# Placing the first instruction of the attention and convolution loops at slot 0 of a fetch line, on every engine

## The reference

```
x = x + attention(gn(x))     # 8x8 windows, 4 heads of 32, keys from the 12x12 around each window,
                             # relative position terms, mask that keeps every second row and column
x = x + conv3x3(gn(x)) + bias   # 128 -> 128 channels, over tiles that aren't all (nearly) zero

qkv = einsum('bchw,oc->bohw', x, W_qkv)
attn = softmax(q k^T + rel_pos_emb(q) + FIXED_MASK)
out = einsum('bchw,oc->bohw', attn v, W_out)
```

## Time and profile before

| | us |
|---|---|
| median of three runs | 3842.27 |
| the profiled execution | 3843.86 |
| its span, first to last instruction | 3842.0 |
| PE busy | 3535.2 |
| DVE busy | 3338.5 |
| ACT busy | 2977.3 |
| POOL busy | 2575.5 |

### The profile page before, as it was taken

The page is one execution under the profiler, slowest core; times in us unless marked ns, Lnnn a source line. Parts: engine busy times, 40 slices in busy tenths (PEclk is TensorE's granted clock), DMA queues, the critical chain, the costliest instruction groups (busy, mean ns, idle before and its releaser), DMA issues. The chain is left out here.

```text
span 3842.0 us, 136271 instructions
## 1 busy us (share of the span) xinstructions
PE 3535.2 (92%) x51718; PEld 2514.5 (65%) x51718; DVE 3338.5 (87%) x5626; ACT 2977.3 (77%) x5320; POOL 2575.5 (67%) x3344
## 2 busy tenths in 40 slices
PE   0799999999999999999999999999949999999999
PEld 0577777777877777777777777778724444444444
DVE  9699999999988888888888888889879888888887
ACT  0788888888988888887888888789657777777774
POOL 1677777777767777776777777677646666666664
PEclk9999999999999999999999999999979999999999
DMA  8344444443333333333333333333234333343332
GB/s 360 82 127 153 138 139 153 128 149 101 96 91 84 94 94 84 99 93 86 85 94 98 83 96 93 85 85 98 75 123 161 147 153 153 147 152 153 151 151 87
DMA packets 492422, 463.06 MB, mean 121 GB/s; under 512 B 9664, under 2 KB 469312, under 8 KB 469440
## 3 DMA queue, kind: packets, MB, share of 16 engines
q1 hardware_dynamic: 491968, 455.92, 36.9%
HBM read 321.40 MB, written 134.48 MB: 119 GB/s over the span
## 5 line engine op out<-in xcount | busy, mean ns | idle before, releaser
L1003 POOL TENSOR_TENSOR sb_tf<-sb_cf 128x1024 f32<-128x1024 f32 x256 | 609.4, 2382 | 393.2 <-DVE sb_tl L985 371.0
L482 PEld LDWEIGHTS ps_s<-sb_kf,sb_qb 128*64 128x64 f32 x16384 | 534.4, 141 | 262.2 <-issue 247.2
L482 PE MATMUL ps_s<-sb_kf,sb_qb 128*64 128x54 f32 x16384 | 601.6, 228 | 91.3 <-issue 88.9
L462 PE MATMUL ps_t<-sb_ident,sb_d 128*108 128x128 f32 x4096 | 671.7, 287 | 8.7 <-ACT sb_pt L650 4.4
L612 DVE TENSOR_TENSOR sb_qb<-ps_q,sb_own_head 128x1024 f32<-128x1024 f32 x512 | 620.6, 1212 | 14.4 <-PE ps_q L444 14.4
L911 PE MATMUL ps_c<-sb_th,sb_wc_h 128*128 128x512 f16 x1536 | 584.7, 381 | 40.3 <-DVE sb_tl L985 40.3
L731 POOL TENSOR_TENSOR sb_erel<-sb_brel 128x288 f32<-128x288 f32 x512 | 351.7, 687 | 375.1 <-DVE sb_brel L559 374.3
L911 PE MATMUL ps_c<-sb_th,sb_wc_l 128*128 128x512 f16 x1536 | 583.8, 380 | 0.0
L911 PE MATMUL ps_c<-sb_tl,sb_wc_h 128*128 128x512 f16 x1536 | 583.7, 380 | 0.0
L738 POOL TENSOR_TENSOR sb_d<-sb_scores,sb_srcp 128x288 f32<-128x288 f32 x512 | 342.8, 670 | 318.3 <-PE ps_t L462 159.3
L761 POOL TENSOR_TENSOR sb_zl<-sb_zf,sb_zh 128x396 f16<-128x396 f32 x512 | 481.2, 940 | 83.7 <-ACT sb_zh L714 82.3
(11 more groups left out here) (117 smaller groups left out, 8258.4 us busy)
## 6 DMA issues: line engine op xcount, KB each, us to landing
sb_xb<-rows SPq DMA_DIRECT2D x128, 780.0 KB, 6.1
sb_xc<-x SPq DMA_DIRECT2D x64, 1280.0 KB, 5.4
sb_x<-rows SPq DMA_DIRECT2D x128, 512.0 KB, 4.0
x<-sb_x SPq DMA_DIRECT2D x128, 512.0 KB, 3.2
out<-sb_oc SPq DMA_DIRECT2D x64, 1024.0 KB, 3.9
sb_abuf<-rows SPq DMA_DIRECT2D x16, 2048.0 KB, 12.4
sb_st<-rows SPq DMA_DIRECT2D x32, 1024.0 KB, 8.6
sb_raw<-wconv SPq DMA_DIRECT2D x1, 576.0 KB, 4.1
```

What stands on the lines that cost most here:

```text
L462: last = pe.transpose(ps_t[0:KV, wj * 128:(wj + 1) * 128], d[:, at:at + KV], ident[:])
L482: last = pe.matmul(s_at, qb[:, qc:qc + QB], kf[:, kc:kc + KR], start=True, stop=True)
L1003: pool.tensor_tensor(tf[:, k * TF:(k + 1) * TF], view(cf, 0, 128, c0 + ra * W, [[2 * W, PAIRROWS], [1, W]]), view(cf, 0, 128, c0 + rb * W, ...
```

## The change

Both helpers pass one more argument to their loops. [...] No other instruction is added, removed or reordered. The untouched lines below it move by one or two in the file.

```diff
-                    with eng.bass.Fori(0, turns, engines=[eng.engine], hint_back_edge=True) as i:
+                    with eng.bass.Fori(0, turns, engines=[eng.engine], hint_back_edge=True,
+                                      head_slot={eng.engine: 0}) as i:
...
-                with eng.bass.Fori(0, CTURNS, engines=[eng.engine], hint_back_edge=True) as i:
+                with eng.bass.Fori(0, CTURNS, engines=[eng.engine], hint_back_edge=True,
+                                      head_slot={eng.engine: 0}) as i:
```

## The result

The changed kernel took 3731.6 us (median of 4 runs, 3729.6 to 3732.0) against 3842.2 us (4 runs, 3834.6 to 3848.4): ratio 0.9712, 95% interval 0.9694 to 0.9730. The forecast was 3720, its range 3706 to 3752. The profiled execution's span is 3729.5 us, 112.5 less than before, where the prediction had 122.5.

The account below looks back on a forecast made before the run. TensorE was taken as the bound, broken by its second-loop branch. Terms -128.3 (second loop), -4 (first loop), +8.8 (exits), +1 (entries) sum to -122.5: 3843.86 to 3721.4, less 1.6 for the profiled run: 3720 us, range 3706 to 3752.

Parts of the forecast that it names:

- What bounded the kernel: Second attention loop: TensorE sets the pace, broken only by 19 pauses at its closing branch, 87.6 us.
- the full value: Second loop, PE: all 320 groups run clean, 1544.5 us instead of 1672.8, so -128.3 us; bounds -60 and -128.3.
- The mechanism: PE's closing branch: the hinted fetch needs line time before it; slot 230 gives about 5.8 us, some 2.5 us sufficed.
- First loop, PE: First attention loop: 8.2 us of pauses before ps_o go, half counted because VectorE is as full: -4 us.
- Leaving the loops: Behind each loop's last branch PE pauses about 5.3 us; net +8.8 us over both exits, bounds +2 and +13.
- Entering: Loop entries: jumping over up to 255 empty slots once per loop and engine, +1 us in all.
- A: Line behind the head comes late, PE still pauses 1.2 us a turn: 3743 to 3781 us, middle 3755, chance 0.12.
- B: Whole kernel: nothing happens, 3842 us, chance 0.04.
- C: Both attention loops: the head's slot decides, not the branch's, so slot 0 stalls both: 3897 us, chance 0.04.
- D: First loop gives all its 8.2 us and the exits' 8.8 us hide: 3707 us, chance 0.06.

Follow-up runs that it names:

- PE alone: Changed kernel with heads at slot 0 on TensorE only, the other four engines as before the change: 3726.9 us, ratio 0.9683.
- slot 4: Changed kernel with TensorE's head at slot 30 in both attention loops, so both closing branches stand 4 instructions into their line: 3882.1 us, ratio 1.0085.
- no hint: Changed kernel without the back-edge hint on TensorE's two attention loops, heads still at slot 0: 3876.8 us.
- all but PE: Changed kernel with heads at slot 0 on every engine except TensorE: 3850.0 us, ratio 1.0002.
- slots 40, 60, 100: Three runs: changed kernel with TensorE's second-loop head at slot 40, 60 or 100: 3851.3, 3853.6 and 3807.6 us.
- the load first: Changed kernel with SyncE issuing the sb_st load ahead of the sb_xb load: 3701.5 us, ratio 0.9626; with slot 0 on TensorE only, 3698.7 us.
- second loop only: Changed kernel without head_slot on the first attention loop; the second and the convolution keep it: 3732.5 us, ratio 0.9698.
- before with the load first: Kernel before the change with only the sb_st load issued ahead of the sb_xb load: 3832.0 us, ratio 0.9960.
- PE's second loop only with the load first: Changed kernel with only TensorE's second-loop head at slot 0 and the sb_st load issued ahead of sb_xb: 3716.4 us, ratio 0.9660.

## Why the prediction was right, and the term that failed

**What bounded the kernel: right.** In the second loop PE was the bound and its branch the only break. Removing the 19 pauses gave 128.1 us, where the sum had 128.3 (1672.8 less 1544.5). 87.6 us of it are the pauses, and 40.7 follow them: the 32 passes behind a pause took 1.96 us instead of 1.14 and the first group 6.99 instead of 4.83, and the windows view has the granted clock at 0.50 from 1061.3 to 1064.7 us. The assumption behind the full value, that neither VectorE nor ScalarE would take over, held: no wait of PE for another engine from 991 to 2536 us.

**The mechanism: right, its reading of time too simple.** PE alone carries it; slot 4 brings it into the first loop; no hint brings it into both. The head's packet starts 4.8 us ahead of the branch at slot 230 and 2.5 us behind it at slot 4, and a late branch ends some 2.5 us after that start, the time that the prediction had read from one exit. That the hint gets the head fetched ahead is shown by the pair with the branch at slot 230: 4.81 us ahead of it with the hint, 2.42 us behind it without. A taken branch took 4.93 and 6.04 us without the hint, 5.0 us with the hint and 4 to 34 instructions into its line, and 0.45 and 0.36 us with 96 and 230. But the prediction's wording that 230 instructions give "5.8 us against some 2.5 us" suggested a price that falls evenly from slot 0 on. It stays at 5.0 us up to 34 instructions.

**The step that failed: "First loop, PE ... I count half: -4".** It measured +5.9, 9.9 of the 10 us by which the sum missed. The 8.2 us of ps_o pauses went, and gave nothing: with PE alone at slot 0 the loop took 659.7 us against 659.3. I had argued from the busy shares that VectorE was as full as PE, and split the difference. The waits would have told it: VectorE itself lay idle 24.3 us for `sb_st` in that loop, and with its busy time that is all but 5.5 us of the loop. Held by VectorE and its transfer, this loop gave nothing for a shorter PE. With the load moved, the same slot gave 14 to 24 us. So the gain was there and hidden behind the transfer.

**The +6 itself** stays open. In the rows it is VectorE's wait for `sb_st`, 30.6 us instead of 24.3. With the other engines' heads at slot 0 (changed kernel, all but PE, slots 40, 60, 100) the first loop took 665.2, 668.1, 658.9, 662.2 and 661.3 us, and 659.3, 659.7 and 661.0 where they were not. The means, 663.1 and 660.0, are no further apart than single executions scatter. One candidate is SyncE, which issues `sb_st`: at the loop's entry its first hint starts at 232.9 us instead of 229.2. It does not explain the 6 us by itself. In the runs with slots 40, 60 and 100 that hint starts at 232.9 to 233.5 too, and the waits for `sb_st` are 24.2, 27.6 and 26.7 us. In medians the other engines' slots cost 2.8 us with the load first (3701.5 against 3698.7).

**Leaving the loops: right in kind, sizes exchanged.** Forecast was a pause of 5.3 us at each exit; measured 4.96 and 3.30. The first exit was to count +1.5 of it, but the written-out units took 5.3 us more, PE's own 2.8 us of longer pause among them; with PE alone at slot 0 they took 3.9 more. VectorE did not hide it. Behind the second loop it was +3.8 instead of +7.3. There the fetch of the next line started 2.54 us after the last branch, and 3.78 behind the first loop; the prediction had taken 4.0 for both, from the first loop's exit. The clock was granted at 0.50 behind either (902 to 908 and 2540.2 to 2543.5 us). Both with the entries: +9.5 against 9.8, so that the exits and entries came out right in sum by luck.

**Entering: +1 forecast, +0.4 measured ahead of the first loop,** but not for every slot. No run shows the empty slots of the prediction's +1; what the runs show is the jump, one branch more per padded loop. It has a price of its own: 0.31 us from about slot 164 or 194, 0.6 to 2.8 us from about slot 122 (the first loop's entry, nine runs), 5.14 and 6.18 us from about slot 30. That the changed kernel's second jump stands at slot 164 is luck; the bounds of the prediction, three pauses of 5, had room for it.

**The rivals.** A, a late line behind the head, did not come: ps_s starts 77.24 us apart over the back edge. Its margin was wider than the half microsecond of the prediction, since in the second loop the line behind the head is fetched 2.1 to 3.7 us after the branch (median 2.5), which makes it usable after some 5.0 us and not 6.6. (The prediction puts A's middle at 3755; the middle of 3743 and 3781 is 3762. And 128.3 us over 19 pauses are 6.75, not 6.6. Neither moves the forecast.) B fell with the result. C, the head's slot decides, fell with slots 30 to 100: the price goes away as the branch moves deeper into its line, and slot 0, which C would have made the worst head, is the best. Head and closing branch move together in these runs; the jumps into the second loop, 0.31 and 6.18 us to the same slot 0, separate the two, though for a jump without hint. D needed the first loop's 8.2 us.

## What to carry to other kernels

Where a loop body is fetched anew in every turn (here 12 or 13 packets a turn), count the instructions from the start of the fetch line to its closing branch on the engine that sets the pace; up to 34 the branch hint bought nothing here, at 74 a third of the branch's time, at 96 two thirds to nearly all. The head's slot is then the cheapest thing to move (here on PE alone; the other engines' heads gained nothing and cost 2.8 us). Look at the slot of the jump into the loop as well, which moves with every head ahead of it (here from slot 30 to 164, and from 6.18 to 0.31 us). A gain in one loop says nothing of the next: before giving a pause's removal a value, look in that loop's waits for who is last, transfers included. After such a change read the loops again; here a load issued ahead of another was worth twice as much as it had been before.

## What the runs showed of the hardware

- PE's taken branch with hint, by instructions between its line's start and the branch: 4, 14 and 34 took 5.0 us (medians 5.04, 4.97, 5.05), 74 took 3.33, 96 took 0.45 in the first loop before, 230 took 0.36. Without hint it was 4.93 in the second loop and 6.04 in the first. At 96 it varied most between runs, with medians of 0.45, 0.63, 0.99, 1.39 and 1.61 us (before, second loop only, all but PE, before with the load first, PE's second loop only with the load first). In the last two the head's fetch started 1.1 us ahead of the branch instead of 1.8 to 2.3.
- From the start of the fetch to the end of a late branch it is 2.3 to 2.7 us in every run. What makes the hinted fetch start late when the branch is up to 34 instructions in stays open; with the branch 74 in, single taken branches ranged from 1.9 to 4.7 us.
- With the hint and the branch at slot 230 the head's fetch started 4.81 us ahead of the branch in the second loop (changed kernel), without the hint, at the same slot, 2.42 us behind it.
- The hint had a price at the end of a loop: with the branch at slot 230 PE paused once behind it, 3.3 to 5.5 us in every run (4.96 and 3.30 in the changed kernel); without the hint no such pause came there.
- The heads stood where `head_slot` asked: behind the last branch of the second loop PE paused after 12 passes with the head at slot 0, after 88 with it at 100 (3.33 us, before L463 at 2619.53) and after 118 with it at 40 (1.61 us, before L483 at 2663.59). To the end of the branch's line that leaves room for 25, 181 and 241 instructions, two a pass.
- The pauses cost more than their length: 128.1 us went with 87.6 us of pauses; after each of the 19, PE's clock was granted at 0.50 for 3.4 or 6.8 us (and 20 passes took 1.32 us behind the changed kernel's exits, at 0.50 too, where 32 take 1.14 at 1.00). Behind the first loop the granted clock of the whole 93 us stretch was 0.94.
- The convolution loop's 611 PE instructions ran without an instruction packet for PE from 2915 to 3771 us in the kernel before, with branches of 0.22 us.
